# Rotary halves of the attention queries: exchanged by a second matrix product, or by DMAs within SBUF

## The chip, the core and the metric

The kernel runs on one core of one Trainium2 chip. The metric is the device time of one execution in microseconds (us). Engines are named as in the profile: PE (TensorE), DVE (VectorE), ACT (ScalarE), POOL (GpSimd) and SP (SyncE, which here only issues DMAs).

## What is computed

A block of three layers on x of shape 4 x 512 x 256: half a mixture-of-experts layer, an attention layer with compressed (latent) queries and keys, and the same mixture of experts again. The change lies in the attention:

```
q = rms_norm(x @ wq_a, q_a_norm_w) @ wq_b            # 16 heads of 64 + 64
q_nope, q_pe = q[..., :64], q[..., 64:]
q_pe = reorder(q_pe)                                  # even elements first, then odd
q_pe = q_pe * cos + concat([-q_pe[32:], q_pe[:32]]) * sin
k_pe = the same for the keys, one for all heads
attn = softmax([q_nope, q_pe] . [k_nope, k_pe] * 128 ** -0.5)
out = (attn @ values) @ wo
```

So each head's 64 rotary elements are needed twice: as they are, times cos, and with their halves exchanged (and one half negated), times sin.

## The kernel before

**Stages.** The first expert layer takes about 0 to 267 us, the attention with its preparation to about 790, and the output product, the second routing and the second expert layer the rest. The attention runs over 32 pairs of heads: p = 0 to 31, eight pairs for each of the 4 batches (B = 4, PAIRS = 8, NPAIR = 32). A pair has 8 tiles k: head k % 2, and rows k // 2 of 4 blocks of 128 queries. The next batch's rows, latents and keys are prepared piece by piece within the pairs of the current one: what is done depends on p % 8 (j in the code), and there is none in the last eight pairs.

**One tile.** PE forms the scores (L1747 to L1749, three matmuls into bank k % 4), DVE takes the negated maximum of each row (L1387), ACT the exponential (L918, with an instruction that reads the row sums behind it), PE transposes the result (four transposes, L1759, into bank 4 + k % 2), and DVE (tiles 0, 1, 4, 5, 7; L1419) or ACT (tiles 2, 3, 6; L927) copies it to SBUF. Behind tile 1 of each pair PE does the attend step of the pair before: 32 matmuls at L1786. DVE copies its result (L1410) behind it. All engines run a program written out in order: in step k of `pair`, PE transposes tile k and forms the scores of tile k + 3, ACT does the exponential of tile k + 2, DVE the maximum of tile k + 3 and the copy of tile k. Tiles 0 to 2 of the next pair thus have their scores in steps 5 to 7.

**The queries.** `queries(p, par, part)` (L1720) on PE forms one of three products of pair p, each by two matmuls (L1734, L1735), in bank 7 for p > 0: part 0 the rotary part, part 1 the same with its halves exchanged (its weights hold the columns in that order, one half negated), part 2 the latent part. For p > 1 part 0 is formed in step 3 of pair p - 2, part 1 in step 6, part 2 in step 0 of pair p - 1. Parts 0 and 1 are freed for the next by DVE's products: `ropes(p, 0)` (L1394, part 0 times cos, in step 4 of pair p - 2, to ropeA) and `ropes(p, 1)` (L1397, part 1 times sin, in step 7, to ropeB). POOL adds them (`rope_sum`, L653), ACT rounds the sum to the matmul's type for each head (`queries_rope`, L938, step 1 of pair p - 1), and POOL takes what the rounding left (`rope_lower`, L662). PE's scores of pair p, tile 0 wait for that (L1741). POOL's `load_weights` (L643, L646) splits the query weights of a pair, three parts of 128 columns, into a rounded and a remaining part.

**The sums.** The inverse of the row sums goes, transposed, to ACT (L943), by SP to HBM (L516), and back, spread over 64 partitions for each head (L519); this is `spread`. POOL multiplies the attended result with it (L672), and SP stores it (`store`, L512). SP runs store(p), then spread(p + 2), in one loop.

**Preparation.** In pairs with p % 8 = 1, 2, 5 and 6, PE turns or projects rows or keys behind the query product of step 3 (and, but for 6, again in step 6), and ACT copies the result at the head of step 4 (L867, L873, L884), and again in step 7. In p % 8 = 5 the second turning of keys waits for DVE's subtraction from the first (L1332, `lower_keys`, at the end of step 5). In p % 8 = 0, 3 and 7 DVE has statistics in step 3 (L1285, L1300, L1280), ahead of `ropes(p + 2, 0)`; in 0, 3 and 4 POOL has extra work.

Of the kernel before, what the change touches and what calls it, by code (L numbers as in the profile page):

```python
# [20 lines left out]
F32 = mybir.dt.float32  # L21
# [3 lines left out]
ALU = mybir.AluOpType  # L25
# [70 lines left out]
def constants():  # L96

    c = np.zeros((P, C_ALL), np.float32)
    c[:, C_ID:C_ID + P] = np.eye(P)
    c[:, C_UP:C_UP + P] = np.triu(np.ones((P, P)), 1)  # L100
    c[:, C_ONE:C_ONE + P] = 1.0
    c[:, C_IOTA:C_IOTA + E] = np.arange(E)
    c[:, C_BASE:C_BASE + E] = np.arange(E) * REGION
    c[:, C_J:C_J + TILES] = np.arange(TILES)
    c[:, C_STEP:C_STEP + NT] = np.arange(NT) * P
    c[:, C_HALF:C_HALF + NT] = -0.5
    c[:, C_LAND:C_LAND + TILES] = 16 * ((np.arange(TILES) - 1) // 3)
    cos, sin = rope_tables()
    c[:, C_KCOS:C_KSIN] = cos.reshape(GT, P, HALF).transpose(1, 0, 2).reshape(P, -1)
    c[:, C_KSIN:C_COS] = sin.reshape(GT, P, HALF).transpose(1, 0, 2).reshape(P, -1)  # L110
    c[:, C_COS:C_SIN] = np.tile(cos.T, (4, 1))
    c[:, C_SIN:C_ALL] = np.tile(sin.T, (4, 1))
    ids = (np.arange(NT)[None, :] * P + np.arange(P)[:, None]).astype(np.int32)
    return c, ids

# [15 lines left out]
def build(nc, x_in, wq_a, qn_w, wq_rope, wq_in, wkv_a, kvn_w, wk_in, wv_in, wo, gate, w0, w1, wout, const, ids_in, out):  # L131
# [6 lines left out]
    with ctx:  # L138
# [48 lines left out]
        def area(at, shape, parts=P):  # L187
            n = int(np.prod(shape))
            v = shared[0:parts, at:at + n]
            names = "abcd"[:len(shape)]  # L190
            return v.rearrange(f"p ({' '.join(names)}) -> p {' '.join(names)}", **dict(zip(names, shape)))
# [104 lines left out]
        cqn = late[:, m:m + GT * P].rearrange("p (t n) -> p t n", t=GT)  # L296
        m += GT * P
        rt = [late[:, m + k * GT * HALF:m + (k + 1) * GT * HALF].rearrange("p (t n) -> p t n", t=GT) for k in range(4)]
        attl = [late[:, 0:PAIRS * S].rearrange("p (a n) -> p a n", a=PAIRS), area(F32_SHARED, [PAIRS, S])]
        x2group = [wlo_plain[:, 2 * B * S + k * GT * D:2 * B * S + (k + 1) * GT * D].rearrange("p (a n) -> p a n", a=GT)  # L300
                   for k in range(2)]
# [34 lines left out]
        k_high, k_low, v_kept = sem("keys_high"), sem("keys_low"), sem("values_kept")  # L336
        wc_high, wcur_ready = (sem(f"query_weights_{k}") for k in ("high", "ready"))
        qa_psum, qb_psum, qz_psum = sem("qa_psum"), sem("qb_psum"), sem("qz_psum")
        ropeA_sb, ropeB_sb, rope_ready = sem("ropeA_sb"), sem("ropeB_sb"), sem("rope_ready")
        qz_high, qz_low, rope_high, rope_low = sem("qz_high"), sem("qz_low"), sem("rope_high"), sem("rope_low")  # L340
        s_psum, max_ready, exp_ready = sem("s_psum"), sem("max_ready"), sem("exp_ready")
# [63 lines left out]
        def _(sp):  # L405
# [105 lines left out]
                sp.wait_ge(att_ready, p + 1)  # L511
                sp.dma_start(atd[p * P:(p + 1) * P, :], att[par]).then_inc(att_stored[par], 16)  # L512

            def spread(p, par):
                sp.wait_ge(invT_sb, p + 1)
                sp.dma_start(invd[p:p + 1, :].rearrange("a (k q) -> (a k) q", k=8), invT).then_inc(inv_stored, 16)  # L516
                sp.wait_ge(inv_stored, (p + 1) * 16)
                for hh in range(2):
                    sp.dma_start(inv[par][hh * HD:(hh + 1) * HD], invd[p:p + 1, hh * S:(hh + 1) * S].to_broadcast([HD, S])).then_inc(inv_in[par], 16)  # L519
# [3 lines left out]
                sp.dma_start(xprep[0][:, 2 * k:2 * k + 2, :], first_rows[:, 2 * k:2 * k + 2, :]).then_inc(x_in_sem[2 * k], 16)  # L523
            for g in range(1, 3):
                load_prep(g)
            spread(0, 0)
            spread(1, 1)
            load_prep(3)
            for p in range(NPAIR - 4):
                store(p, p % 2)  # L530
                spread(p + 2, p % 2)

            def load_x(g):
                if g > 1:
# [15 lines left out]
            load_x(1)  # L550
            for p in (NPAIR - 4, NPAIR - 3):
                store(p, p % 2)
                spread(p + 2, p % 2)
            sp.wait_ge(o_psum, NPAIR)
            load_attended(1)
            for p in (NPAIR - 2, NPAIR - 1):
# [17 lines left out]
        def _(pool):  # L574
# [62 lines left out]

            def load_weights(p, par):

                src = wpair[:, p % PAIRS, :, :]  # L640
                if p > 1:
                    pool.wait_ge(qz_psum, p - 1)
                nc.gpsimd.tensor_copy(wch[par], src).then_inc(wc_high, 1)  # L643
                pool.wait_ge(wc_high, p + 1)
                pool.sem_inc(pool_issue, 1)
                nc.gpsimd.tensor_tensor(wcl[par], src, wch[par].bitcast(F32), ALU.subtract).then_inc(wcur_ready, 1)  # L646

            def rope_sum(p):

# [131 lines left out]
        def _(act):  # L781
# [148 lines left out]
            def queries_latent(p, par, hh):  # L930
                act.wait_ge(qz_psum, p + 1)
                rows_ = (slice(HD, P), slice(0, HD))[hh]
                nc.scalar.copy(qh[par][hh][rows_], query_bank(p, 2)[rows_, :]).then_inc(qz_high, 1)

            def queries_rope(p, par, hh):
                act.wait_ge(rope_ready, p + 1)
                rows_ = (slice(0, HD), slice(HD, P))[hh]
                nc.scalar.copy(qh[par][hh][rows_], rope[rows_]).then_inc(rope_high, 1)  # L938
# [6 lines left out]
            def pair(p, par):  # L945
                first, last = p == 0, p == NPAIR - 1
                b, j = p // PAIRS + 1, p % PAIRS
                for k in range(8):
                    s = p * 8 + k
                    if b < B and k == 4:  # L950
                        if j == 1:
                            rows_out(b, 0, 6)
                        elif j == 2:
                            latents_out(b, 0, 6)
                        elif j == 5:
                            high_keys(b, 0, 6)
                        elif j == 6:
                            high_keys(b, 2, 6)
                    if not (last and k > 5):
                        exp(s + 2, k + 2, par if k < 6 else 1 - par, first and k < 2)  # L960
                    if b < B and k == 7:
                        if j == 1:
                            rows_out(b, 1, 6)
                        elif j == 2:
                            latents_out(b, 1, 6)
                            squares(b)
                        elif j == 5:
                            high_keys(b, 1, 6)
                    if k in BY_ACT:
                        copy_pT(p, par, k)  # L970
                    if k == (3 if first else 0) and not last:
                        for hh in range(2):
                            queries_latent(p + 1, 1 - par, hh)
                    if k == (4 if first else 1) and not last:
                        for hh in range(2):
                            queries_rope(p + 1, 1 - par, hh)
                    if k == 2 and not first:
                        take_inverse(p - 1)
# [32 lines left out]
        def _(dve):  # L1011
# [252 lines left out]
            for two in range(2):  # L1264
                src = rope_w[:, :, :, two:ROPE:2]
                for hh in range(2):
                    at = hh * HD
                    V.tensor_scalar(wpair[:, :, 0, at + two * HALF:at + (two + 1) * HALF], src[:, :, hh, :],
                                    norm_w[:, 0:1], None, ALU.mult)
                    last = V.tensor_scalar(wpair[:, :, 1, at + (1 - two) * HALF:at + (2 - two) * HALF], src[:, :, hh, :],  # L1270
                                           norm_w[:, 0:1], -1.0 if two else 1.0, ALU.mult, ALU.mult)
            last.then_inc(wa_ready, 1)


# [114 lines left out]
            def ropes(p, which):  # L1389
                if which == 0:  # L1390
                    dve.wait_ge(qa_psum, p + 1)
                    if not among(p, 0):
                        dve.wait_ge(rope_ready, p)
                    V.tensor_tensor(ropeA, query_bank(p, 0)[:, :], qcos, ALU.mult).then_inc(ropeA_sb, 1)  # L1394
                else:
                    dve.wait_ge(qb_psum, p + 1)
                    V.tensor_tensor(ropeB, query_bank(p, 1)[:, :], qsin, ALU.mult).then_inc(ropeB_sb, 1)  # L1397

            def latent_lower(p, par, hh):
                rows_ = (slice(HD, P), slice(0, HD))[hh]  # L1400
# [25 lines left out]
            def pair(p, par):  # L1426
                first, last = p == 0, p == NPAIR - 1
                for k in range(8):
# [4 lines left out]
                        invert_sums(p - 1, 1 - par)  # L1433
                    if k == (5 if first else 4) and not among(p, NPAIR - 2, NPAIR - 1):
                        ropes(p + 2, 0)
                    if k == 7 and not among(p, NPAIR - 2, NPAIR - 1):
                        ropes(p + 2, 1)
                    if k in BY_DVE:
                        copy_pT(p, par, k)
                    if k == (4 if first else 1) and not last:  # L1440
# [61 lines left out]
        def _(pe):  # L1502
# [217 lines left out]
            def queries(p, par, part):  # L1720

                src = cq[:, p // PAIRS, :]
                if part == 0:
                    pe.wait_ge(wcur_ready, p + 1)
                    if p % PAIRS == 0:
                        pe.wait_ge(k_low, p // PAIRS * 3 + 2)
                    if not among(p, 0):
                        pe.wait_ge(qz_low, p * 2)
                    if not among(p, 0, 1, 2):
                        pe.wait_ge(invT_sb, p - 2)  # L1730
                elif not among(p, 0):
                    pe.wait_ge((ropeA_sb, ropeB_sb)[part - 1], p + 1)
                to = query_bank(p, part)
                mm(to[:, :], wch[par][:, part, :], src, start=True, stop=False)  # L1734
                mm(to[:, :], wcl[par][:, part, :], src, start=False, stop=True)\  # L1735
# [58 lines left out]
            def pair(p, par):  # L1794
                first, last = p == 0, p == NPAIR - 1
                b, j = p // PAIRS + 1, p % PAIRS
                for k in range(8):
# [17 lines left out]
                    if k == 3 and b < B:  # L1815
# [6 lines left out]
                            turn_keys(b, 0, 6)  # L1822
                        elif j == 6:
                            turn_keys(b, 2, 6)
                    if k == 6 and p + 2 < NPAIR:
                        queries(p + 2, par, 1)
                    if k == 6 and j in (1, 2, 5):
                        bank_back(b, j, 0)
                        if b < B and j == 1:
# [80 lines left out]
```

## Time and profile before

| | us |
|---|---|
| median of 3 runs | 1088.32 (1087.28 to 1092.0) |
| the profiled execution | 1089.1 |
| its span, first to last instruction | 1087.3 |
| PE busy | 1015.2 (93%) |
| DVE busy | 734.1 (68%) |
| ACT busy | 518.0 (48%) |
| POOL busy | 477.7 (44%) |

Busy times are shares of the whole span, over stages with different limits; which engine sets the end of one stage has to be read within it. Matmuls are pipelined: a record of PE is longer than the step to the next one, so the steps are read from starts. A "releaser" is the instruction whose end ended an engine's idle time.

### The profile page before, as it was taken

The numbers are of one execution on the slowest core, as the hardware profiler recorded it, in microseconds if no ns is written. First come the engines' busy times: TensorE is split into PE (matmuls) and PEld (weight loads), VectorE is DVE, ScalarE is ACT, GpSimd is POOL, SyncE is SP. The second block draws the span as 40 slices with busy tenths as digits, with TensorE's granted clock in tenths as the row PEclk, the third lists the DMA queues.
The fourth block names the chain that finished last, engine by engine and source line by source line (L and its number), as shares of the span: only waits on it lengthen the run. The fifth ranks groups of instructions, "written<-read, shape, count | busy, mean of one in ns | idle before, by whom it ended". The sixth has DMA issues, their size and how long they took to land.

```text
span 1087.3 us, 22878 instructions
## 1 busy us (share of the span) xinstructions
PE 1015.2 (93%) x6183; PEld 803.4 (74%) x6184; DVE 734.1 (68%) x1677; ACT 518.0 (48%) x1133; POOL 477.7 (44%) x418
## 2 busy tenths in 40 slices
PE   5569999999889999999999999999999889999995
PEld 4448888887558777777778777777788558888884
DVE  7725666745577788877887788788556845766642
ACT  2213334422366676767767677777411214443421
POOL 3723443433343644645463644443125514443422
PEclk9979999999899999999999999999999989999998
DMA  9836455431101101111011110111567545544330
GB/s 330 217 112 158 103 114 136 81 49 26 58 1 49 40 22 40 40 40 40 21 40 40 40 39 23 39 40 40 182 216 241 178 117 116 160 109 110 48 58 7
DMA packets 72098, 95.66 MB, mean 88 GB/s; under 512 B 9840, under 2 KB 49008, under 8 KB 71984
## 3 DMA queue, kind: packets, MB, share of 16 engines
q1 hardware_dynamic: 56560, 76.76, 22.4%
q0 software_dynamic: 14304, 16.87, 9.2%
q10 hardware_dynamic: 1152, 1.06, 0.4%
q8 instruction: 38, 0.62, 0.3%
q14 instruction: 44, 0.36, 0.1%
HBM read 64.14 MB, written 34.43 MB: 91 GB/s over the span
## 4 chain that ended last, share of the span: by engine, by line
PE 86%; DVE 8%; issue 2%; ACT 1%; DMA 1%; POOL 1%; POOLq 0%; SPq 0%; DVEq 0%; ACTq 0%
PE bank L1759 11%; PE bank L1786 11%; PE bank L1576 7%; PE bank L1574 7%; PE bank L1578 7%; PE bank L1747 5%; PE bank L1749 5%; PE bank L1748 5%; PE bank L1859 4%; PE bank L1586 4%; PE bank L1588 3%; PE bank L1587 3%; PE bank L1559 3%; PE bank L1734 2%; PE bank L1735 2%
## 5 line engine op out<-in xcount | busy, mean ns | idle before, releaser
L918 ACT ACTIVATE shared<-bank,small 128x512 f32<-128x512 f32 x256 | 176.5, 690 | 90.9 <-DVE small L1387 89.9
L1387 DVE TENSOR_REDUCE small<-bank 128x1 f32<-128x512 f32 x256 | 174.5, 684 | 41.7 <-PE bank L1749 41.6
L835 ACT CAST split_rows_and_inner<-bank 128x512 fp32r<-128x512 f32 x78 | 45.8, 587 | 237.8 <-PE bank L1559 237.8
L1759 PE MATMUL bank<-constants,shared 128*128 128x128 f32 x1024 | 156.3, 275 | 2.3 <-ACT shared L918 0.7
L1759 PEld LDWEIGHTS bank<-constants,shared 128*128 128x128 f32 x1024 | 122.3, 141 | 44.9 <-issue 13.9
L1576 PE MATMUL bank<-expert_weights_low,split_rows_and_inner 128*128 x312 | 144.3, 463 | 0.0
L1578 PE MATMUL bank<-expert_weights_high,split_rows_and_inner 128*128 x312 | 143.4, 460 | 0.0
L1574 PE MATMUL bank<-expert_weights_high,split_rows_and_inner 128*128 x312 | 125.4, 402 | 2.5 <-DVE split_rows_and_inner L1166 2.5
L1747 PE MATMUL bank<-expert_weights_high,shared_split 128*128 128x512 f32 x256 | 122.5, 479 | 2.4 <-POOL shared_split L662 1.4
L653 POOL TENSOR_TENSOR shared<-shared 128x512 f32<-128x512 f32 x32 | 41.2, 1289 | 188.9 <-DVE shared L1397 185.5
L1171 DVE TENSOR_TENSOR split_rows_and_inner<-bank,split_rows_and_inner 128x512 fp32r<-128x512 f32 x78 | 53.9, 692 | 103.9 <-ACT split_rows_and_inner L835 103.9
L619 POOL DMA_INDIRECT out<-shared,small x39 | 61.3, 1571 | 132.3 <-DVE shared L1190 75.2
L619 POOL DMA_INDIRECT x_after_moe<-shared,small x39 | 62.3, 1598 | 129.3 <-DVE shared L1190 84.9
L1786 PE MATMUL bank<-shared 128*64 128x256 f32 x1024 | 117.6, 382 | 0.1
L1419 DVE COPY shared<-bank 128x512 f32<-128x512 f32 x160 | 109.3, 683 | 8.8 <-PE bank L1759 7.4
L1786 PEld LDWEIGHTS bank<-shared 128*64 128x64 f32 x1024 | 71.2, 137 | 43.4 <-issue 11.6
L1749 PE MATMUL bank<-expert_weights_high,shared_split 128*128 128x512 f32 x256 | 101.2, 395 | 0.0
L1748 PE MATMUL bank<-expert_weights_low,shared_split 128*128 128x512 f32 x256 | 100.4, 392 | 0.0
L1586 PE MATMUL bank<-expert_weights_high,split_rows_and_inner 128*128 x312 | 89.6, 287 | 3.0 <-DVE split_rows_and_inner L1171 3.0
L1588 PE MATMUL bank<-expert_weights_high,split_rows_and_inner 128*128 x312 | 88.1, 282 | 0.0
L662 POOL TENSOR_TENSOR shared_split<-shared,shared_split 64x512 fp32r<-64x512 f32 x63 | 80.0, 1269 | 18.5 <-ACT shared_split L938 12.7
L1587 PE MATMUL bank<-expert_weights_low,split_rows_and_inner 128*128 x312 | 88.0, 282 | 0.0
(201 smaller groups left out, 2190.1 us busy)
## 6 DMA issues: line engine op xcount, KB each, us to landing
expert_weights<-w SPq DMA_DIRECT2D x32, 512.0 KB, 4.5
shared<-rows_by_expert SPq DMA_DIRECT2D x78, 129.0 KB, 2.1
expert_weights<-wo SPq DMA_DIRECT2D x16, 512.0 KB, 6.8
shared<-inverse_sums SPq DMA_DIRECT2D x64, 128.0 KB, 2.9
attended_transposed<-shared SPq DMA_DIRECT2D x32, 256.0 KB, 3.1
expert_weights<-attended_transposed SPq DMA_DIRECT2D x2, 2048.0 KB, 10.0
shared<-attended_transposed SPq DMA_DIRECT2D x2, 2048.0 KB, 10.4
expert_weights_low_plain<-x_after_moe SPq DMA_DIRECT2D x4, 512.0 KB, 9.0
```

The costliest lines, as they stand in the source:

```text
L619: nc.gpsimd.indirect_dma_start(out=dst, out_offset=bass.IndirectOffsetOnAxis(ap=tag[:, t, 1:2].bitcast(U32), axis=0), in_=ysb[v], in_offse ...
L918: nc.scalar.activation(prob[k % 4], bank[k % 4][:, :], ACT.Exp, bias=negmax[:, k % 8:k % 8 + 1], accum_out=psum[par][:, hh * GT + qt:hh * ...
L1387: V.tensor_reduce(negmax[:, k % 8:k % 8 + 1], bank[k % 4][:, :], AX.X, ALU.max, negate=True).then_inc(max_ready, 1)
L1574: mm(b[:, :], high, whi[:, bass.ds(w, MLP)], start=(c == 0), stop=False)
L1576: mm(b[:, :], high, wlo[:, bass.ds(w, MLP)], start=False, stop=False)
L1578: last = mm(b[:, :], low, whi[:, bass.ds(w, MLP)], start=False, stop=(c == KC - 1))
L1586: mm(bank[7][:, 0:D], interTh[:, c, :], whi[:, bass.ds(w, D)], start=(c == 0), stop=False)
L1747: mm(bank[k % 4][:, :], q_high, high, start=True, stop=False)
L1748: mm(bank[k % 4][:, :], q_high, low, start=False, stop=False)
L1749: mm(bank[k % 4][:, :], q_low, high, start=False, stop=True).then_inc(s_psum, 1)
L1759: last = tr(bank[4 + k % 2][:, c * P:(c + 1) * P], prob[k % 4][:, c * P:(c + 1) * P], ident)
L1786: last = mm(bank[6][hh * HD:(hh + 1) * HD, half * 2 * P:(half + 1) * 2 * P].rearrange("p (t n) -> p t n", t=2), values[:, p // PAIRS, c, : ...
```

## The change

For the pairs p = 2 to 31 the second product isn't formed. ACT copies part 0 as it is from bank 7 to a new SBUF area, `unturned` (`queries_unturned`, at step 4 of pair p - 2, or 5 in pair 0; behind the preparation's copy and ahead of the exponential of that step). SP then sends it by four DMAs of 32 partitions, 64 KB each, into ropeB, with the halves exchanged (`turn_queries`). `spread` is split into `inverse_out` and `inverse_back`, and the four DMAs stand between them. DVE's `ropes(p, 0)` also waits for ACT's copy; `ropes(p, 1)` waits for the DMAs, works in place on ropeB, and stands in step 0 of pair p - 1, ahead of DVE's copy of tile 0, where it stood in step 7 of the pair before. The sign of the exchanged half is now in the table of sines, and the weights of part 1, without the sign, are kept for pairs 0 and 1 alone; POOL's `load_weights` handles two parts in place of three from p = 2 on.

```diff
-    c[:, C_SIN:C_ALL] = np.tile(sin.T, (4, 1))
+    c[:, C_SIN:C_ALL] = np.concatenate([-sin.T, sin.T, -sin.T, sin.T])
 ...
+            def turn_queries(p):
+
+                sp.wait_ge(unturned_sb, p - 1)
+                sp.wait_ge(rope_ready, p)
+                for a in range(4):
+                    b = a + 1 - 2 * (a % 2)
+                    sp.dma_start(ropeB[a * HALF:(a + 1) * HALF], unturned[b * HALF:(b + 1) * HALF]).then_inc(turned_in, 16)
 ...
-            spread(0, 0)
-            spread(1, 1)
+            for p in range(2):
+                turn_queries(p + 2)
+                if p == 1:
+                    inverse_back(0, 0)
+                inverse_out(p)
+            turn_queries(4)
+            inverse_back(1, 1)
             load_prep(3)
             for p in range(NPAIR - 4):
                 store(p, p % 2)
-                spread(p + 2, p % 2)
+                inverse_out(p + 2)
+                if p + 5 < NPAIR:
+                    turn_queries(p + 5)
+                inverse_back(p + 2, p % 2)
 ...
             def load_weights(p, par):
 
-                src = wpair[:, p % PAIRS, :, :]
+                parts_ = slice(0, 3) if among(p, 0, 1) else slice(0, 3, 2)
+                src = wpair[:, p % PAIRS, parts_, :]
 ...
+            def queries_unturned(p):
+                act.wait_ge(qa_psum, p + 1)
+                if not among(p, 2):
+                    act.wait_ge(turned_in, (p - 2) * 64)
+                nc.scalar.copy(unturned, bank[7][:, :]).then_inc(unturned_sb, 1)
 ...
+                    if k == (5 if first else 4) and p + 2 < NPAIR:
+                        queries_unturned(p + 2)
                     if not (last and k > 5):
                         exp(s + 2, k + 2, par if k < 6 else 1 - par, first and k < 2)
 ...
                     if not among(p, 0):
                         dve.wait_ge(rope_ready, p)
+                    if not among(p, 0, 1):
+                        dve.wait_ge(unturned_sb, p - 1)
                     V.tensor_tensor(ropeA, query_bank(p, 0)[:, :], qcos, ALU.mult).then_inc(ropeA_sb, 1)
                 else:
-                    dve.wait_ge(qb_psum, p + 1)
-                    V.tensor_tensor(ropeB, query_bank(p, 1)[:, :], qsin, ALU.mult).then_inc(ropeB_sb, 1)
+                    if among(p, 0, 1):
+                        dve.wait_ge(qb_psum, p + 1)
+                        turned = query_bank(p, 1)[:, :]
+                    else:
+                        dve.wait_ge(turned_in, (p - 1) * 64)
+                        turned = ropeB
+                    V.tensor_tensor(ropeB, turned, qsin, ALU.mult).then_inc(ropeB_sb, 1)
 ...
-                    if k == 7 and not among(p, NPAIR - 2, NPAIR - 1):
-                        ropes(p + 2, 1)
+                    if k == 0 and not first and not last:
+                        ropes(p + 1, 1)
 ...
-                    if k == 6 and p + 2 < NPAIR:
-                        queries(p + 2, par, 1)
```

## Rows read from the trace of the kernel before

**Rows 1.** Stages: stretch and length, busy time (and instructions) by engine, clock, DMA.
```profile
290.00:840.00 550.00, 540.74 (x3456) 418.06 (x3457) 420.59 (x842) 344.89 (x814) 260.77 (x261) 0.99 0.18 59
...
327.06:342.24 15.18, 15.18 (x106) 11.82 (x104) 11.89 (x19) 11.09 (x26) 6.68 (x7) 1.00 0.06 19
342.24:359.16 16.92, 16.92 (x113) 13.62 (x112) 11.89 (x19) 11.61 (x27) 6.59 (x7) 1.00 0.21 64
359.16:374.15 14.99, 14.69 (x97) 10.76 (x96) 12.19 (x21) 10.09 (x24) 9.88 (x12) 1.00 0.12 37
...
388.46:403.72 15.26, 15.26 (x106) 11.76 (x104) 13.08 (x21) 11.20 (x26) 6.58 (x7) 1.00 0.11 35
524.75:539.48 14.73, 14.73 (x101) 11.38 (x99) 12.12 (x20) 10.64 (x25) 6.35 (x7) 1.00 0.11 38
539.48:554.35 14.87, 14.71 (x98) 10.82 (x96) 12.63 (x23) 10.09 (x24) 6.20 (x7) 1.00 0.11 37
554.35:569.06 14.71, 14.56 (x97) 10.77 (x96) 11.89 (x24) 10.10 (x24) 11.57 (x11) 1.00 0.12 37
674.88:689.19 14.31, 14.31 (x97) 10.96 (x96) 11.47 (x19) 10.10 (x24) 6.53 (x7) 1.00 0.11 39
```
**Rows 2.** Timeline, pair 24: start, length, engine, line, operation, out<-in, idle before.
```profile
677.31 0.40 PE L1734 MATMUL bank<-expert_weights_high,shared_split 128*128 128x512 f32 x1
...
677.68 0.58 ACT L927 COPY shared<-bank 128x512 f32<-128x512 f32 x1
677.78 0.60 PE L1759 MATMUL bank<-constants,shared 128*128 128x128 f32 x4
...
678.12 0.68 DVE L1394 TENSOR_TENSOR shared<-bank,constants 128x512 f32<-128x512 f32 x1
...
678.24 0.69 ACT L918 ACTIVATE shared<-bank,small 128x512 f32<-128x512 f32 x1
...
681.63 0.60 PE L1759 MATMUL bank<-constants,shared 128*128 128x128 f32 x4
...
681.90 0.58 ACT L927 COPY shared<-bank 128x512 f32<-128x512 f32 x1
...
682.76 0.60 PE L1759 MATMUL bank<-constants,shared 128*128 128x128 f32 x4
682.82 1.29 POOL L653 TENSOR_TENSOR shared<-shared 128x512 f32<-128x512 f32 x1 [7.31 <-DVE shared L1397]
...
687.14 2.68 POOL L662 TENSOR_TENSOR shared_split<-shared,shared_split 64x512 fp32r<-64x512 f32 x2
```
**Rows 3.** Timeline, pair 3 (from 359.16) and pair 16 (from 554.35).
```profile
363.18 0.69 DVE L1394 TENSOR_TENSOR shared<-bank,constants 128x512 f32<-128x512 f32 x1
...
367.70 0.63 PE L1759 MATMUL bank<-constants,shared 128*128 128x128 f32 x4 [0.16 <-ACT shared L927]
...
558.08 0.69 DVE L1394 TENSOR_TENSOR shared<-bank,constants 128x512 f32<-128x512 f32 x1
...
562.59 0.63 PE L1759 MATMUL bank<-constants,shared 128*128 128x128 f32 x4
```
**Rows 4.** Timeline, pair 2 (from 342.24) and pair 13 (from 509.47).
```profile
346.63 0.48 ACT L873 COPY expert_weights<-bank 128x384 f32<-128x384 f32 x1 [1.02 <-PE bank L1698]
...
348.69 0.60 PE L1759 MATMUL bank<-constants,shared 128*128 128x128 f32 x4
...
513.02 0.59 ACT L884 CAST expert_weights_high<-bank 128x512 fp32r<-128x512 f32 x1 [0.17 <-PE bank L1706]
...
513.50 0.70 ACT L918 ACTIVATE shared<-bank,small 128x512 f32<-128x512 f32 x1
...
515.95 0.68 DVE L1332 TENSOR_TENSOR expert_weights_low<-bank,expert_weights_high 128x512 fp32r<-128x512 f32 x1
```
**Rows 5.** The line of the attended store: duration of issue, and time to landing.
```profile
L512 SPq DMA_DIRECT2D attended_transposed<-shared x32: 319/584/1506, 347.0 to 787.8; - x32
...
DMA to landing us min/median/max: 2.9/3.1/11.5
```

More of the change, by code:

```diff
@@ L298, in build @@
         rt = [late[:, m + k * GT * HALF:m + (k + 1) * GT * HALF].rearrange("p (t n) -> p t n", t=GT) for k in range(4)]
+        m += 4 * GT * HALF
+        unturned = late[:, m:m + S]
         attl = [late[:, 0:PAIRS * S].rearrange("p (a n) -> p a n", a=PAIRS), area(F32_SHARED, [PAIRS, S])]
@@ L338, in build @@
         qa_psum, qb_psum, qz_psum = sem("qa_psum"), sem("qb_psum"), sem("qz_psum")
+        unturned_sb, turned_in = sem("queries_unturned"), sem("queries_turned")
         ropeA_sb, ropeB_sb, rope_ready = sem("ropeA_sb"), sem("ropeB_sb"), sem("rope_ready")
@@ L512, in store, with inverse_out, inverse_back @@
                 sp.dma_start(atd[p * P:(p + 1) * P, :], att[par]).then_inc(att_stored[par], 16)
-            def spread(p, par):
+            def turn_queries(p):
[4 more added lines that the diff above has]
+                    sp.dma_start(ropeB[a * HALF:(a + 1) * HALF], unturned[b * HALF:(b + 1) * HALF]).then_inc(turned_in, 16)
+            def inverse_out(p):
                 sp.wait_ge(invT_sb, p + 1)
                 sp.dma_start(invd[p:p + 1, :].rearrange("a (k q) -> (a k) q", k=8), invT).then_inc(inv_stored, 16)
+            def inverse_back(p, par):
                 sp.wait_ge(inv_stored, (p + 1) * 16)
@@ L552, in _ @@
                 store(p, p % 2)
-                spread(p + 2, p % 2)
+                inverse_out(p + 2)
+                inverse_back(p + 2, p % 2)
             sp.wait_ge(o_psum, NPAIR)
@@ L638, in load_weights @@
             def load_weights(p, par):
-                src = wpair[:, p % PAIRS, :, :]
+                parts_ = slice(0, 3) if among(p, 0, 1) else slice(0, 3, 2)
+                src = wpair[:, p % PAIRS, parts_, :]
                 if p > 1:
                     pool.wait_ge(qz_psum, p - 1)
-                nc.gpsimd.tensor_copy(wch[par], src).then_inc(wc_high, 1)
+                nc.gpsimd.tensor_copy(wch[par][:, parts_, :], src).then_inc(wc_high, 1)
                 pool.wait_ge(wc_high, p + 1)
                 pool.sem_inc(pool_issue, 1)
-                nc.gpsimd.tensor_tensor(wcl[par], src, wch[par].bitcast(F32), ALU.subtract).then_inc(wcur_ready, 1)
+                nc.gpsimd.tensor_tensor(wcl[par][:, parts_, :], src, wch[par][:, parts_, :].bitcast(F32),
+                                        ALU.subtract).then_inc(wcur_ready, 1)
             def rope_sum(p):
@@ L1269, in _ @@
                                     norm_w[:, 0:1], None, ALU.mult)
-                    last = V.tensor_scalar(wpair[:, :, 1, at + (1 - two) * HALF:at + (2 - two) * HALF], src[:, :, hh, :],
-                                           norm_w[:, 0:1], -1.0 if two else 1.0, ALU.mult, ALU.mult)
+                    last = V.tensor_scalar(wpair[:, 0:2, 1, at + (1 - two) * HALF:at + (2 - two) * HALF], src[:, 0:2, hh, :],
+                                           norm_w[:, 0:1], None, ALU.mult)
             last.then_inc(wa_ready, 1)
@@ L1730, in queries @@
                         pe.wait_ge(invT_sb, p - 2)
+                elif among(p, 1):
+                    pe.wait_ge((ropeA_sb, ropeB_sb)[part - 1], p + 1)
                 elif not among(p, 0):
-                    pe.wait_ge((ropeA_sb, ropeB_sb)[part - 1], p + 1)
+                    pe.wait_ge(ropeA_sb, p + 1)
                 to = query_bank(p, part)
```

## Prediction

> **What bounds the kernel now.** I read the table of stages first. In the attention stage, 290 to 840 us, TensorE is busy 540.74 of 550.00 us at a granted clock of 0.99, with DVE at 420.59 and ACT at 344.89 [rows 1]. So on average this stage belongs to TensorE. Then I cut it at the moment at which a pair's third tile is transposed (tile 2; the long attend step of the pair before has just ended), because all engines have caught up there: DVE's copy of the attended result waits for TensorE at that point in every pair. I call this moment t = 0 and count all times of a pair from it; a dash marks tiles of the next pair. The lengths from one t = 0 to the next are 14.31 us for a pair without preparation work, and 14.71 to 16.92 with it [rows 1]. By p modulo 8 the windows shown are 1, 2, 3, 5, 6, 7, 0, and pair 24, a plain one.
>
> Then I read the timeline of pair 24, t = 0 at 674.88. ACT's copy of transposed tile 3 starts at 2.80, its next instruction (the exponential of tile 6) at 3.36; DVE's first rotary product starts at 3.24; ACT's copy of tile 6 at 7.02, and the transposes of tile 0' at 7.88 [rows 2]. Tiles 6 and 0' share a PSUM bank, so 0' waits for that copy. It is ready at 7.02 + 0.58 + about 0.15 = 7.75: **the slack is 0.13 us**. The whole chain is: first product, DVE's copy of tile 4, maximum 7, copy of tile 5, maximum 0', then ACT's exponential 0', copy of tile 6, then TensorE. DVE and ACT run it back to back.
>
> Other pairs show what happens when the first product starts late, because DVE has preparation work in front of it. Pair 16 (t = 0 at 554.35): product at 3.73, tile 0' at 8.24, length 14.71. Pair 3 (359.16): product at 4.02, tile 0' at 8.54, length 14.99. Pair 15 (row statistics in the same place): length 14.87 [rows 1, 3]. So tile 0' starts at product + 4.51 as soon as this is over 7.88, and the length is that start + 6.43 (14.31 - 7.88; 6.47 and 6.45 in the two with rows). The late start is not recovered behind the attend step.
>
> **The change, part by part.** (1) Removed: the turned query product of pairs 2 to 31, two matmuls like those of the query product, 677.31 to 677.78, that is 0.47 us [rows 2]. 30 x 0.47 = 14.1 us of TensorE, all of it in its queue ahead of tile 7.
>
> (2) Added: ACT copies the untouched queries from PSUM, 128x512, 30 times. A copy of that shape takes 0.58 [rows 2]; ACT has room for it in total. Its place is behind the copy of tile 3 and ahead of exponential 6. The query product ends where tile 4's transposes start, 677.78, at 2.90, plus about 0.2 of drain: 3.10. ACT comes free at 3.36 [rows 2]. So the copy runs 3.36 to 3.94.
>
> (3) Added wait: DVE's first product, at 3.24 now, waits for that copy. It starts at 3.94 + 0.04 = 3.98, that is 0.74 later. Behind it on DVE are queued copy 4, maximum 7, copy 5, maximum 0'; ACT and then TensorE wait for these. By the rule just read, tile 0' starts at 3.98 + 4.51 = 8.49 and the pair lasts 14.92: **+0.61 against 14.31**. The 0.47 us removed ahead of tile 7 doesn't help, since tile 0' doesn't wait for TensorE any more. Without the removal the pair would last as long.
>
> (4) The second product goes from tile 7 of one pair to tile 0' of the next; its time from SBUF is taken as that of the first product. It is behind maximum 2', at about 8.8 (eight instructions at 0.60 behind the first product), and no part of the chain above stands behind it. GpSimd's sum, at 7.94 now, goes to about 9.5; it has been idle for 7.31 us there. Its last work on these queries ends at 689.82 [rows 2], 0.63 behind the next t = 0, and goes to 0.63 + 1.6 - 0.6 = 1.6. The first scores that need it stand at about 4.4 (two tile steps of 1.13, a product and a set of scores ahead of 7.88): over 2 us are left. GpSimd's smaller weights shorten this. Cost 0, as long as the DMAs land.
>
> (5) Four DMAs on SP's queue behind the inverse's store and ahead of its spread, each of 64 KB. The trace has no DMA within SBUF. The nearest: the attended store, 584 ns of issue at the median and 3.1 us to landing [rows 5]. Issued from 3.98, the last at 3.98 + 3 x 0.58 = 5.7, landed at 8.8: just where DVE asks. The bound from below is fewer rows per issue (319 ns), landed at 8.0; from above the longest landing, 11.5 us, at 17. I take 3.1 us. The spread is late by 1.3 to 2.3 us; its product is made by GpSimd after the sum, at 10.8, which covers that. By the Trainium skill ("SBUF — State Buffer", The DMA setup-cost knee) a DMA costs some 2 us plus its bytes, which would land them before 8.8 and speaks against the late-DMA rival below; no row of this trace shows such a DMA. The same page (Who interferes with whom) says that a DVE instruction with two SBUF inputs contends with GpSimd instructions that read SBUF, which is new for the second product. It would hold one of them by at most its 0.68 us, and only where GpSimd has preparation work; the slack of (4) covers that.
>
> (6) The pairs by kind. Plain (4, 12, 20, 23 to 29): 10 x 0.61 = 6.1. Kind 0 (8, 16): the product goes from 3.73 to 3.98, 2 x 0.25 = 0.5. Kind 7 (7, 15): its 14.87 answers to a product at 3.93 (14.87 - 6.43 - 4.51), so 2 x 0.05 = 0.1. Kind 3: the product is at 4.02 already, 0. In the kinds 1, 2, 5 and 6 ACT takes a preparation copy ahead of the new one. In kind 5 this is at 513.02, 3.55 from 509.47, and the next instruction starts 0.48 later [rows 4]; kinds 1 and 6, with a copy of the same shape behind four transposes of the same kind, are taken alike. There the new copy runs 4.03 to 4.61, the product starts at 4.65, tile 0' at 9.15, and the pair lasts 15.57: kind 6, 14.73 now, +0.83, three times 2.5; kind 1, 15.18 now, +0.38, 1.1. Kind 5 has a second link: TensorE's turning of the next keys behind tile 6 waits for DVE's lower keys, which start at 6.48 now [rows 4]. With the product at 4.65 and five instructions at 0.60 they start at 7.65 and end at 8.33. Then keys 8.4 to 8.9, tile 7 and a set of scores 1.13 (681.63 to 682.76 [rows 2]), so tile 0' is at 10.03 and the pair at 16.46 against 15.26: +1.20, three times 3.6. Kind 2: ACT's copy starts at 346.63, 4.39, and the new one at 4.76; the product at 5.38, tile 4 copied at 6.75, where tile 6 starts at 6.45 now [rows 4]. TensorE is otherwise the bound: +0.30 - 0.47 = -0.17, three times -0.5. Pair 0 (start-up, waits of its own) I leave at 0, within half a us.
>
> Sum: 6.1 + 0.5 + 0.1 + 2.5 + 1.1 + 3.6 - 0.5 = **+13.4 us**. The profiled execution took 1089.1 (span 1087.3); the median of the three shown is 1088.3. 1089.1 + 13.4 = 1102.5; on the median 1101.7. The constants and the shorter weight preparation ahead of the loop stand beside other waits: 0.
>
> **Rivals.** (A) The wait costs nothing and TensorE's 14.1 us come off: 1088.3 - 14.1 = 1074.2. For it: TensorE is busy 98% of the stage. Against: the slack of 0.13 us, and the pairs 3 and 16, in which a late product makes a longer pair. 0.07. (B) Only the plain pairs and kind 0 lose, since in the prepared pairs TensorE's extra work and what is removed give room that I did not see: +6.1 + 0.5 - 0.5 - some of the rest, 1094 at most, about 1091. For it: their lengths before are above 15 for TensorE's sake. Against: the ACT copy ahead of the new one. 0.10, counted as no change. (C) The DMAs land late. The path: second product, sum, ACT's rotary copy, which blocks exponential 4' behind it, then TensorE. It decides from some 3 us after 8.8, that is at a landing of 6 us; every us more costs 29 us, so 1130 for one. For it: the 11.5 us seen once. Against: the median of 3.1 and engines that are 11% busy here [rows 1]. 0.07. (D) The change doing nothing at all isn't possible: 60 matmuls go.
>
> **The numbers.** Forecast 0.76, with its own range 1095 to 1108 (0.1 us more or less at each of 26 pairs is 2.6 us; kind 5's link carries 3.6). The range for 8 in 10 also takes in the upper part of B and a little of C: 1092 to 1110. A measurement here tells 0.5%, 5.4 us, from no change. Slower by more 0.82 (forecast, less its lowest edge, and C), within 0.10, faster 0.08.
>
> **What would show it.** Right: in plain pairs DVE's first product about 4.0 after t = 0, tile 0' at 8.5, with TensorE idle for 0.5 to 1 us ahead of tile 7 or tile 0' and ACT's copy as its releaser; lengths 14.9 (plain), 16.4 (kind 5), 16.75 (kind 2); SP's four issues by 6 and landed by 9; GpSimd's sum at 9.5. Wrong: a first product before 3.7, a plain pair under 14.3, or DVE's second product waiting on a DMA for over 3 us.

## The result, and the profile after

| | us |
|---|---|
| median before, same chip | 1089.49 (4 runs, 1087.28 to 1092.0) |
| median after | 1106.99 (4 runs, 1105.26 to 1107.15) |
| ratio | 1.0163, 95% interval 1.0142 to 1.0184 |
| profiled execution after | span 1105.2 |

The changed kernel is slower by 1.6%, about 17.5 us; 13.4 had been forecast, and the range held the time.

In the same stretch of time, 290 to 840 us, PE is now busy for 523.23 us where it was for 540.74 [rows 1]; it gets less far in it, as the pairs last longer. The first fence is the table of stretches after: the stage, then pairs 2, 3, 5 and 25 from t = 0 to the next t = 0; the columns are those of [rows 1].

```profile
290.00:840.00 550.00, 523.23 (x3301) 387.73 (x3302) 408.62 (x769) 353.89 (x838) 239.86 (x252) 0.99 0.22 66
...
344.32:361.28 16.96, 16.65 (x111) 13.15 (x110) 11.62 (x19) 11.88 (x28) 5.88 (x6) 1.00 0.28 79
361.28:376.32 15.04, 14.47 (x96) 10.36 (x94) 12.23 (x21) 10.40 (x25) 9.92 (x13) 1.00 0.19 54
391.28:407.80 16.52, 15.13 (x103) 11.30 (x102) 13.10 (x21) 11.02 (x26) 4.82 (x6) 1.00 0.16 48
703.64:718.62 14.98, 14.49 (x96) 10.37 (x94) 11.53 (x19) 10.40 (x25) 6.11 (x7) 1.00 0.18 54
```

The plain pair was PE from end to end, 14.31 of 14.31; now it lasts 14.98 with PE busy 14.49, and its weight loads have gone from 10.96 to 10.37. The clock is at its upper level in both. The pair's timeline shows where the time goes. Pair 25, t = 0 at 703.64:

```profile
706.45 0.58 ACT L951 COPY shared<-bank 128x512 f32<-128x512 f32 x1
706.56 0.60 PE L1800 MATMUL bank<-constants,shared 128*128 128x128 f32 x4
706.91 0.60 ACT L963 COPY expert_weights<-bank 128x512 f32<-128x512 f32 x1
...
707.39 0.71 ACT L942 ACTIVATE shared<-bank,small 128x512 f32<-128x512 f32 x1
...
707.54 2.47 SPq L523 DMA_DIRECT2D shared<-expert_weights  x4
707.64 0.69 DVE L1428 TENSOR_TENSOR shared<-bank,constants 128x512 f32<-128x512 f32 x1 [0.66 <-ACT expert_weights L963]
...
711.44 0.57 ACT L951 COPY shared<-bank 128x512 f32<-128x512 f32 x1
...
712.16 0.63 PE L1800 MATMUL bank<-constants,shared 128*128 128x128 f32 x4 [0.41 <-ACT shared L951]
712.43 0.69 DVE L1436 TENSOR_TENSOR shared<-shared,constants 128x512 f32<-128x512 f32 x1
```

These answer to [rows 2]. Counted from t = 0, ACT's copy for the exchange (L963) starts at 3.27; DVE's first product (L1428) waits 0.66 us for it and starts at 4.00, where it started at 3.24; ACT's copy of tile 6 starts at 7.80 in place of 7.02; tile 0' at 8.52 in place of 7.88, with PE idle before it, released by that copy. The chain that ended last, over the same pair, is the same sequence (start, length, what). It is PE's before 705 and after 712, and in between it goes through the added copy:

```profile
706.91 0.61 ACT expert_weights L963
707.52 0.03 issue
707.55 0.05 DVEq L1427
707.60 0.04 issue
707.64 0.06 DVE shared L1428
707.70 0.55 issue
708.25 0.68 DVE shared L1458
708.93 0.60 DVE small L1419
709.53 0.60 DVE shared L1458
710.13 0.61 DVE small L1419
...
711.44 0.58 ACT shared L951
712.02 0.14 issue
712.16 0.63 PE bank L1800 x4
```

The first product, copy of tile 4, maximum 7, copy of tile 5, maximum 0', exponential 0', copy of tile 6: the chain named ahead of the run. L1427 is DVE's wait for ACT's copy, an instruction of its own in DVE's queue.

One table more, made from the starts of DVE's copy of the attended result, one in each pair: the length in us from one t = 0 to the next. A kind is p modulo 8 (plain: a pair without preparation work), the pair shown stands in brackets, and the others of its kind agree with it within 0.06 us. The columns e1 to e8 belong to the next section.

```
kind (pairs)      before after  e2     e3     e5     e6     e1     e4     e7     e8
plain (25)        14.30  14.97  14.97  14.96  14.97  15.57  14.22  14.03  13.83  14.31
0 (8)             14.69  14.98  14.97  14.98  14.97  15.58  14.68  14.12  13.83  14.36
1 (9)             15.20  15.74  15.81  15.72  15.83  16.32  14.72  14.75  14.75  15.17
2 (2)             16.92  16.96  17.41  16.93  17.40  17.60  16.46  16.46  16.46  16.92
3 (3)             15.00  15.04  15.02  15.02  15.03  15.58  15.00  14.40  13.86  14.64
5 (5)             15.26  16.52  16.54  16.54  16.54  17.14  15.26  15.27  15.25  15.25
6 (6)             14.74  15.71  15.71  15.70  15.70  16.32  14.43  14.44  14.27  14.74
7 (7)             14.85  14.98  14.97  14.97  14.96  15.58  14.85  14.25  14.02  14.51
```

Pair 24 alone is off its kind in the changed kernel: 15.33.

### The profile page after: what moved, and what is told of

It reads as the page before. It is cut to its first block, busy times and chain, and to the rows that moved or that the text cites. A ratio compares the mean times of both kernels' runs of the same rounds, so it can differ in the third digit from the quotient of the medians.

```text
span 1105.2 us, 22967 instructions
## 1 busy us (share of the span) xinstructions
PE 1012.1 (92%) x6123; PEld 786.3 (71%) x6124; DVE 737.7 (67%) x1677; ACT 529.1 (48%) x1163; POOL 465.3 (42%) x418
## 4 chain that ended last, share of the span: by engine, by line
PE 72%; DVE 14%; issue 7%; ACT 4%; DMA 1%; another core or an unknown queue 1%; POOL 1%; DVEq 0%; POOLq 0%; ACTq 0%; SPq 0%
PE bank L1827 10%; PE bank L1800 7%; PE bank L1615 7%; PE bank L1613 7%; PE bank L1617 7%; PE bank L1625 4%; PE bank L1898 3%; DVE small L1419 3%; PE bank L1627 3%; PE bank L1626 3%; DVE shared L1458 3%; PE bank L1598 3%; PE bank L1788 3%; PE bank L1790 3%; PE bank L1789 3%
## 5 line engine op out<-in xcount | busy, mean ns | idle before, releaser
L1800 PE MATMUL bank<-constants,shared 128*128 128x128 f32 x1024 | 159.0, 278 | 16.3 <-ACT shared L951 8.7
L1800 PEld LDWEIGHTS bank<-constants,shared 128*128 128x128 f32 x1024 | 118.4, 141 | 75.6 <-ACT shared L942 39.0
L677 POOL TENSOR_TENSOR shared<-shared 128x512 f32<-128x512 f32 x32 | 41.1, 1285 | 234.4 <-DMA shared<-inverse_sums 131.5
L1598 PE MATMUL bank<-constants,shared 128*128 128x128 f32 x312 | 83.8, 272 | 0.3 <-DVE shared L1209 0.2
```

What stands on the lines that cost most here:

```text
L1800: last = tr(bank[4 + k % 2][:, c * P:(c + 1) * P], prob[k % 4][:, c * P:(c + 1) * P], ident)
```

## The experiments

All against the kernel before on the same chip. Theory W is that of the forecast: DVE's wait on ACT's copy delays the chain to tile 0', and the removed product was not on the path. Rival D blames the four DMAs and what is late behind them on SP's queue. Rival C has the removal give its 14 us, and the wait cost twice as much. (These letters are those of the expectations below; the prediction's own rival C, late DMAs, is part of D here.)

**The copy and the wait alone (e2).** On the kernel before:

```diff
+            def queries_unturned(p):
+                act.wait_ge(qa_psum, p + 1)
+                nc.scalar.copy(unturned, bank[7][:, :]).then_inc(unturned_sb, 1)
...
+                    if k == (5 if first else 4) and p + 2 < NPAIR:
+                        queries_unturned(p + 2)
                     if not (last and k > 5):
                         exp(s + 2, k + 2, par if k < 6 else 1 - par, first and k < 2)
...
                         dve.wait_ge(rope_ready, p)
+                    if not among(p, 0, 1):
+                        dve.wait_ge(unturned_sb, p - 1)
```

> The kernel before, with ACT's copy of the untouched queries and DVE's wait for it added, and nothing else: the turned product stays on PE, no DMAs, nothing reads the copy. Theory W (DVE's wait on the copy delays the chain to tile 0' of each pair, and the removed product was not on the path): the whole slowdown of the change is here, 1.016 to 1.018 of before; plain pairs last 14.97 us, kind 5 16.5. Rival D (SP's four DMAs, and the inverse sums that come late behind them, hold POOL and so PE): 1.00 of before. Rival C (the copy costs, but PE's 14 us were saved elsewhere): 1.03, since the product is still formed.

Measured: 1106.05 us against 1088.82, ratio 1.0152 (1.0125 to 1.0179), a little under what was expected, with an interval that covers it. A copy that nobody reads, with a wait for it, costs what the whole change costs, and pair by pair the same but in kind 2 (17.41 against 16.96: there the product still formed counts its 0.47) and kind 1 (0.07 more). Rival D falls, as there are no new DMAs here, and rival C too, as the product is still formed. Its rows in pair 25, t = 0 at 702.19, are those of the changed kernel: the product at 3.99, tile 0' at 8.51.

```profile
705.46 0.60 ACT L940 COPY expert_weights<-bank 128x512 f32<-128x512 f32 x1
...
706.18 0.69 DVE L1405 TENSOR_TENSOR shared<-bank,constants 128x512 f32<-128x512 f32 x1 [0.66 <-ACT expert_weights L940]
...
710.70 0.63 PE L1770 MATMUL bank<-constants,shared 128*128 128x128 f32 x4 [0.15 <-ACT shared L930]
```

**No DMAs (e3).**

```diff
-                for a in range(4):
-                    b = a + 1 - 2 * (a % 2)
-                    sp.dma_start(ropeB[a * HALF:(a + 1) * HALF], unturned[b * HALF:(b + 1) * HALF]).then_inc(turned_in, 16)
...
-                    act.wait_ge(turned_in, (p - 2) * 64)
+                    act.wait_ge(ropeB_sb, p)
...
-                        dve.wait_ge(turned_in, (p - 1) * 64)
-                        turned = ropeB
+                        turned = unturned
```

> The changed kernel without the four DMAs: DVE multiplies ACT's copy as it lies, so the halves aren't exchanged and the result isn't the reference's. Theory W: nothing on the path goes, 1.015 to 1.017 of before, plain pairs 14.97 us. Rival D: most of the 17 us come back, 1.00 of before or less.

Measured: 1103.62 us, ratio 1.0134 (1.0114 to 1.0155), a little under what was expected, with an interval that reaches it. The pairs 1 to 29 are the same as in the changed kernel within 0.06 us each. In the profiles what is lower lies ahead of pair 1, which starts 4.6 us earlier here; behind pair 29 this run is 1.5 us longer. Within the pairs the DMAs cost nothing.

**The product put back (e5).** In step 6, two matmuls of part 0's weights into bank 7, which nobody reads.

```diff
+                    if k == 6 and p + 2 < NPAIR:
+                        idle_product(p + 2, par)
```

> The changed kernel with two matmuls put back on PE at the place of the removed product (part 0 once more, into the same bank; nobody reads it). Theory W: the removal was worth nothing but in kind 2, where PE is the bound: plain pairs still 14.97, kind 2 at 17.4, 1.016 to 1.018 of before. Rival C (the removal gave its 14 us, and the added wait cost 30): 1.028.

Measured: 1106.23 us against 1088.25, ratio 1.0174 (1.0148 to 1.0199). As expected: 60 matmuls more, and no pair is longer but kind 2 (+0.44) and kind 1 (+0.09, which had not been expected).

**The copy made twice (e6).**

```diff
-                nc.scalar.copy(unturned, bank[7][:, :]).then_inc(unturned_sb, 1)
+                own.step(nc.scalar.copy(unturned, bank[7][:, :]))
+                own.settle()
+                nc.scalar.copy(unturned, bank[7][:, :]).then_inc(unturned_sb, 1)
```

> The changed kernel with ACT's copy made twice, the second waiting for the first, and the signal to DVE after the second: the suspected cost doubled, some 0.7 us later for DVE's first product. Theory W: every pair from 1 to 29 longer by 0.65 to 0.7 (kind 2, where PE was nearly the bound, by 0.5 to 0.65), plain 15.65, 1.033 to 1.036 of before. Rival D or any theory in which DVE's first product isn't what counts: the two hundredths of the changed kernel, 1.016 to 1.02.

Measured: 1123.31 us, ratio 1.0316 (1.0292 to 1.034), under the expected 1.033 to 1.036. The dose was smaller than thought: the second copy starts 0.63 behind the first (719.71 and 720.34 below; t = 0 at 716.46), and DVE's product at 4.60, 0.60 later than in the changed kernel. The pairs follow it to the hundredth: plain 15.57 for 14.97, +0.60.

```profile
719.71 0.60 ACT L963 COPY expert_weights<-bank 128x512 f32<-128x512 f32 x1
720.34 0.59 ACT L965 COPY expert_weights<-bank 128x512 f32<-128x512 f32 x1
...
721.06 0.69 DVE L1430 TENSOR_TENSOR shared<-bank,constants 128x512 f32<-128x512 f32 x1 [1.29 <-ACT expert_weights L965]
...
725.57 0.63 PE L1802 MATMUL bank<-constants,shared 128*128 128x128 f32 x4 [0.41 <-ACT shared L951]
```

**DVE first (e1).** Both read bank 7, and the order between them is turned; no kernel without any order was tried.

```diff
             def queries_unturned(p):
-                act.wait_ge(qa_psum, p + 1)
+                act.wait_ge(ropeA_sb, p + 1)
...
-                    if not among(p, 0, 1):
-                        dve.wait_ge(unturned_sb, p - 1)
...
-                    if k == (5 if first else 4) and p + 2 < NPAIR:
-                        queries_unturned(p + 2)
                     if not (last and k > 5):
                         exp(s + 2, k + 2, par if k < 6 else 1 - par, first and k < 2)
+                    if k == (5 if first else 4) and p + 2 < NPAIR:
+                        queries_unturned(p + 2)
...
                 elif not among(p, 0):
                     pe.wait_ge(ropeA_sb, p + 1)
+                    pe.wait_ge(unturned_sb, p - 1)
```

> The changed kernel with the order of the two readers of bank 7 turned round: DVE's first product doesn't wait, ACT's copy waits for the product and stands behind the exponential of its step; PE's latent product waits for the copy. Theory W: the first product starts at 3.24 again, tile 0' at 7.75 in plain pairs, which last 14.18; pairs of kinds 1, 2 and 6 are 0.47 shorter than before, kinds 0, 3, 5, 7 as before. Together some -5.5 us, +0.8 for the start: 0.995 to 0.997 of before. Rival D: the DMAs start 0.6 us later still, so no better than the changed kernel, 1.016.

Measured: 1081.96 us, ratio 0.9948 (0.9931 to 0.9965). The same DMAs, the same copy, the same matmuls as the changed kernel, and 25 us less. Of PE's 0.47 us a plain pair keeps 0.08 (0.07 to 0.16 over the ten); there the chain is still the bound, as its slack before was only 0.13. Kinds 1 and 2 keep all of it, as expected; kind 6 keeps 0.31 of the expected 0.47. ACT's copy also moved behind the exponential here, so this run alone doesn't tell the wait from the copy's place on ACT; the next one does.

**The product in step 7 (e4).**

```diff
-                    if k == (5 if first else 4) and not among(p, NPAIR - 2, NPAIR - 1):
+                    if k == 7 and not among(p, NPAIR - 2, NPAIR - 1):
                         ropes(p + 2, 0)
```

> The changed kernel with DVE's first product moved from step 4 to step 7, where the second stood before the change; the copy is where it is and the wait is kept, but is over by then. Theory W: the chain to tile 0' loses one DVE instruction of 0.60 as well as the wait; tile 0' at 7.55 in plain pairs (14.0 us), kinds 0, 3 and 7 at 14.1 to 14.4, kinds 1, 2, 6 shorter than before by 0.47, kind 5 as before: some -11 us, 0.989 to 0.992 of before. Rival D: no better than the changed kernel, 1.016. Rival P (PE's work is not what ends the pair even then): 0.995 to 1.00.

Measured: 1078.02 us, ratio 0.9891 (0.9862 to 0.992). One line more than the change, which moves the instruction that has to wait behind those for which PE waits: 29 us under the changed kernel. ACT's copy is where the change put it, 3.27 from t = 0 in pair 25, and the plain pair lasts 14.03, as expected with that copy at no cost: what had cost time was DVE's wait, not ACT's work.

**And ACT's copy of tile 6 first (e7).** On e4; the same edit on the kernel before is e8.

```diff
+                    if k == 6:
+                        copy_pT(p, par, k)
                     if not (last and k > 5):
                         exp(s + 2, k + 2, par if k < 6 else 1 - par, first and k < 2)
...
-                    if k in BY_ACT:
+                    if k in BY_ACT and k != 6:
                         copy_pT(p, par, k)
```

> The kernel with the first product in step 7, and in addition ACT copies transposed tile 6 ahead of the exponential of tile 0 of the next pair, not behind it. Theory W: the last link of the chain to tile 0' goes too, so PE alone ends the plain pairs: 13.84 (14.31 less 0.47), kinds 0, 3 and 7 at 13.9, kind 5 as before; 0.984 to 0.987 of before. Rival: the exponential of tile 0', now later, takes the copy's place: 0.989 as without it.

> The kernel before with ACT's copy of tile 6 ahead of the exponential of tile 0 of the next pair, and nothing of the change. Theory W: plain pairs stay at 14.31, since PE ends them; kinds 0, 3 and 7, where DVE's statistics make the chain late, go to 14.3: some -4 us, 0.995 to 0.998 of before. Rival: the order there doesn't matter, 1.00.

Measured: e7 1070.74 us, ratio 0.9842 (0.9821 to 0.9862); e8 1084.41 us, 0.9958 (0.9943 to 0.9974). In e7 the plain pair is again all PE's, and shorter by the whole product; pairs 2, 3, 5 and 25:

```profile
337.60:354.06 16.46, 16.46 (x110) 13.24 (x111) 11.80 (x19) 12.11 (x28) 6.29 (x7) 1.00 0.28 81
354.06:367.92 13.86, 13.86 (x94) 10.49 (x95) 12.18 (x22) 10.19 (x24) 8.84 (x12) 1.00 0.20 59
381.75:397.00 15.25, 14.93 (x102) 11.36 (x103) 13.18 (x21) 11.46 (x28) 5.89 (x7) 1.00 0.17 52
671.51:685.34 13.83, 13.83 (x94) 10.58 (x95) 11.61 (x19) 10.61 (x26) 6.31 (x7) 1.00 0.21 58
```

Kind 5 alone keeps a wait (PE busy 14.93 of 15.25), that on DVE's lower keys. e8 gains in the kinds 0, 3 and 7 only, where DVE's statistics had made the chain late; they stop at 14.36, 14.64 and 14.51, not at the expected 14.3. In e7, too, kind 7 stays at 14.02, 0.2 above the plain pairs, where 13.9 was expected; why was not looked into. By the ratios, 17.2 us of e7 and 4.6 of e8, some 12.6 us of e7 need the change. By the lengths of the pairs 1 to 31 in the profiles, which leave out what varies ahead of them, e7 gains 16.2 us and e8 3.0, so 13.2 need it. Either way, exchanging by DMA is worth most of PE's 14 us once the order lets it be.

## Why the prediction was right

**The bound.** It came from a stretch in which PE was busy all the time and the clock full, which reads as PE-bound. The slack of 0.13 us between the last copy and tile 0' was right: e1 takes away the wait and keeps the removal, and a plain pair gains 0.07 to 0.16 of 0.47.

**The wait.** The product was put at 3.98 and stood at 4.00, by two errors that cancel, of which below; tile 0' at 8.49 and stood at 8.52; the plain pair at 14.92 and lasted 14.97. PE sat idle ahead of tile 0' for 0.41 us, a little less than the 0.5 to 1 that had been named. The rule read from pairs 3 and 16 [rows 3], tile 0' = product + 4.51, holds in after (4.52), e2 (4.52) and e6 (4.51).

**The removal.** Nothing but in kind 2: e5 and e2 show it.

**The DMAs.** Issue was 0.59 us each at the median (2.47 for the four of pair 25) and landing 2.0 us at the median (1.9 to 3.2), where 3.1 had been taken from the attended store [rows 5]. The Trainium skill ("SBUF — State Buffer", The DMA setup-cost knee) gives about 2 us for what doesn't depend on the bytes, and this trace agrees. The order of the queue cost nothing, as said: e3. DVE's second product from two SBUF inputs took 685 ns at the median (681 to 693, 30 times), and from PSUM 680 at the median before.

**Contention with GpSimd.** The prediction allowed for it, at 0.68 us at most and at no cost. It is there in two pairs of the changed kernel, 8 and 16, at 0.53 and 0.55 us; they are no longer than the plain ones. The last section has the rows.

**What was too small.** The pairs 1 to 29 give +16.2 us, the sum said 13.4. By kind, the missing 2.8 us are 0.7 in the plain pairs (0.4 of them in pair 24 alone), 0.5 in kind 1, 0.4 in kind 6, 0.65 in kind 2, 0.2 in kind 5 and 0.3 in kinds 0, 3 and 7. One term was mis-sized everywhere: from the end of ACT's copy to DVE's start there are 0.13 us, not the 0.04 assumed (706.91 + 0.60 = 707.51 to 707.64), and 0.05 of them are the wait instruction L1427. In the plain pairs this doesn't show, by luck: the copy was put at 3.36 to 3.94 and ran 3.27 to 3.87, so two errors of 0.09 and 0.07 us cancel. In kinds 1, 5 and 6 the copy ran where it was put, and the product stood at 4.73 to 4.76 for 4.65. In kind 2 it was at 5.51 (349.83 from 344.32) for 5.38, with tile 6 at 6.95 for 6.75 and so 16.96 for 16.75. The 0.36 us of pair 24 are in all kernels that keep this wait (after, e2, e3, e5: 15.32 or 15.33; e6 15.93) and in none of the others; DVE's product starts 0.48 behind the copy's end there. What holds it stays open.

**Ahead of pair 1** lie 1.5 us more that the forecast had at 0. In the profiles the pair begins anywhere from 322.9 to 328.7 (by DVE's copy) in the ten kernels of this study, in no order that follows their edits, so nothing ties this to the change; 0.8 of it falls in the stretch of lower clock described below. With 16.2, 1.5 and 0.2 behind pair 29 the profiled spans differ by 17.9 (1087.3 and 1105.2).

**The rivals.** A and B gave PE's 14 us a chance, 0.17 together; e4 and e7 show that most of them can be had, but by an order that the change didn't have. C, late DMAs, was off by 4 us of landing.

The profile names one releaser wrongly. Between 300 and 800 us after the change POOL's sum waits 131.5 us "for" the spread of the inverse sums (us in total, times, longest):

```profile
POOL shared L677 <- DMA shared<-inverse_sums: 131.5, 19, 9.1
POOL shared L677 <- DVE shared L1436: 98.9, 10, 11.5
```

It starts 0.17 us behind the end of DVE's second product in pair 25 (712.43 + 0.69 = 713.12, and 713.29), and the landing of a DMA that it doesn't wait for falls into the same moment. e3, without the four DMAs, has the same pairs.

## What to carry to other kernels

Work taken from a busy engine shortens nothing if another chain ends at the same moment: look for the smallest slack of a wait, not for idle time. An added wait also delays what stands behind it in that engine's queue; put the waiting instruction behind those that others need, and measure the chain on natural cases in the trace before, where the same instruction is late for another reason. Here a move of one line made 1.6% slower into 1.1% faster, and one more made it 1.6%.

## What the runs showed of the hardware

**The clock in pair 0.** PE idles there for 1.8 and, after 1.1 us of work, for 1.4 us in every kernel, and what follows differs from profile to profile (each is of another kernel). Stretches of the kernel before and of the changed one (the column ahead of the last two is the granted clock; 0.50 is the 1.2 GHz level):

```profile
317.00:320.00 3.00, 3.00 (x15) 2.53 (x14) 1.45 (x3) 1.29 (x4) 0.00 (x0) 0.71 0.00 0
320.00:327.20 7.20, 7.20 (x53) 4.95 (x53) 5.56 (x10) 5.27 (x12) 4.84 (x5) 1.00 0.00 0
```
```profile
317.70:322.00 4.30, 4.30 (x15) 3.47 (x14) 2.08 (x3) 2.04 (x5) 0.00 (x0) 0.50 0.13 31
322.00:328.70 6.70, 6.70 (x50) 4.47 (x49) 5.07 (x8) 4.53 (x10) 4.52 (x5) 0.99 0.00 0
```

In the kernel before the lower level lasts from 315.3 to 318.7, in the changed one from 315.3 to 322.1, and from the first scores to t = 0 of pair 1 the changed kernel takes 26.7 us in place of 25.9. These 0.8 us arise between the scores at 318.58 (317.87 before) and the transposes at 322.14 (320.63 before): 3.56 us in place of 2.76, though the turned product is no longer formed there. In e3, e4 and e6 a low phase had come earlier, around pair 0's first scores, and doesn't come back behind these stalls; in e7 the clock doesn't fall in either place. None of this was tested by itself. e3 takes 25.3 us over the same part, 1.4 less than the changed kernel, so single profiles move by a microsecond or so. PE's waits of 0.3 to 1.0 us in the pairs after the change left the clock at 1.00.

**DVE and GpSimd, both reading SBUF.** In the pairs 8 and 16 one of GpSimd's eight normalizing instructions (L719 in the changed kernel, SBUF to SBUF) overlaps DVE's second product, which reads its other input from SBUF after the change and from PSUM before. Which of the two takes longer depends on their starts:

```
kernel   product   starts behind     GpSimd took,   product took,
         reads     GpSimd's, us      us             us
after    SBUF      0.05, 0.07        1.75, 1.77     0.69, 0.69
e3       SBUF      0.04, 0.06        1.74, 1.75     0.68, 0.68
e2       PSUM      0.06, 0.07        1.21, 1.23     0.68, 0.68
e7       SBUF      0.16, 0.19        1.21, 1.23     0.93, 0.91
e4       SBUF      0.18, 0.20        1.21, 1.22     0.91, 0.89
e1       SBUF      0.23, 0.24        1.21, 1.22     0.86, 0.85
e5       SBUF      0.26, 0.28        1.21, 1.22     0.83, 0.81
e6       SBUF      0.67, 0.71        1.21, 1.22     0.68, 0.68
```

In the view of the changed kernel the two are in the maximum (min/median/max in ns):

```profile
L719 POOL TENSOR_SCALAR expert_weights<-expert_weights,small x8: 1215/1226/1773, 443.6 to 572.1; 128x256 f32<-128x256 f32 x8
```

Started nearly together, GpSimd's instruction takes 0.52 to 0.55 us more. Started 0.16 to 0.28 us later, the product takes 0.13 to 0.25 us more, and ends 1.09 or 1.10 us behind GpSimd's start whatever its own. With an input from PSUM at the same distance (e2), neither takes more.
